# Attention + MoE layer on one core: attention's sums turned by VectorE in 32 by 32 blocks instead of by TensorE

## What is computed

```
xn = layernorm(x)
q, k = rope(xn Wq^T), rope(xn Wk^T);  v = xn Wv^T        # 16 heads of width 8
attn = softmax(q k^T / sqrt(8)) v                          # over the 512 keys of a batch
h    = relu(xn up^T)^2 * combine                           # 32 experts of width 64; combine: top 6 of 32
moe  = h down^T;   shared = relu(xn sup^T)^2 sdown^T       # width 256
out  = x + attn + moe + shared
```

## Time and profile before

| | |
|---|---|
| median of 3 runs | 612.33 us (611.86 to 616.31) |
| the profiled execution, its own time | 611.43 us |
| its span in the trace | 609.6 us |
| TensorE busy | 603.1 us (99%) |
| VectorE, ScalarE, GpSimd busy | 425.5, 407.9, 428.4 us |

### The profile page before, as it was taken

The page is one execution under the profiler, slowest core; times in us unless marked ns, Lnnn a source line. Parts: engine busy times, 40 slices in busy tenths (PEclk is TensorE's granted clock), DMA queues, the critical chain, the costliest instruction groups (busy, mean ns, idle before and its releaser), DMA issues.

```text
span 609.6 us, 20168 instructions
## 1 busy us (share of the span) xinstructions
PE 603.1 (99%) x8269; PEld 269.1 (44%) x8269; DVE 425.5 (70%) x1058; ACT 407.9 (67%) x803; POOL 428.4 (70%) x512
## 2 busy tenths in 40 slices
PE   9999999999999999999999999999999999999997
PEld 7432544444444444434444434454443444444343
DVE  7898965777767776677867778586766877666402
ACT  3578667766776666766667676676667666666664
POOL 5850478677896778867788678876776767667653
PEclk9999999999999999999999999999999999999999
DMA  5176743646446254652437454263544634343430
GB/s 149 32 218 200 165 115 88 216 105 158 111 94 206 59 151 111 205 145 70 122 80 243 106 154 104 68 209 85 140 112 145 191 80 113 75 106 71 106 72 18
DMA packets 52029, 76.19 MB, mean 125 GB/s; under 512 B 5985, under 2 KB 19169, under 8 KB 51937
## 3 DMA queue, kind: packets, MB, share of 16 engines
q1 hardware_dynamic: 51916, 74.90, 45.6%
q10 hardware_dynamic: 20, 0.00, 0.0%
HBM read 56.14 MB, written 18.35 MB: 122 GB/s over the span
## 4 chain that ended last, share of the span: by engine, by line
PE 95%; DVE 2%; DMA 1%; SPq 1%; ACT 0%; issue 0%; DVEq 0%
PE acc L1060 21%; PE pv L1227 20%; PE st L1060 15%; PE upb L1060 10%; PE st L1197 9%; PE sc L1186 6%; PE upb L1197 4%; PE st L1202 3%; PE upb L1202 2%; PE sc L1119 1%; PE st L1169 1%; DVE nmax L930 1%; SPq L361 1%; DMA stacks<-k_stack 1%; DMA k_stack<-qk_parts 1%; PE upb L1169 1%
## 5 line engine op out<-in xcount | busy, mean ns | idle before, releaser
L930 DVE TENSOR_REDUCE nmax<-sc 128x1 f32<-128x512 f32 x512 | 328.5, 686 | 142.7 <-PE sc L1186 131.7
L700 ACT ACTIVATE probs<-st 128x512 f32<-128x512 f32 x359 | 202.8, 595 | 29.1 <-PE st L1202 19.3
L558 POOL TENSOR_TENSOR gated<-gate_at,relu 128x512 f32<-128x512 f32 x111 | 142.0, 1280 | 98.3 <-ACT relu L705 92.0
L562 POOL TENSOR_TENSOR g<-gated,relu 128x512 f32<-128x512 f32 x111 | 142.2, 1281 | 16.2 <-POOL gated L558 0.4
L1202 PE MATMUL st<-stacks 32*128 32x512 f32 x359 | 148.6, 577 | 0.0
L1227 PE MATMUL pv<-probs,v_aug 128*32 128x512 f32 x1024 | 136.4, 605 | 0.1
L1060 PE MATMUL acc<-dn,g 128*32 128x128 f32 x3512 | 134.8, 274 | 0.0
L1186 PE MATMUL sc<-stacks 32*128 32x512 f32 x512 | 132.6, 493 | 0.9 <-DMA stacks<-k_stack 0.4
L1060 PEld LDWEIGHTS acc<-dn,g 128*32 128x32 f32 x3512 | 112.2, 114 | 22.3 <-issue 22.1
L700 ACT ACTIVATE probs<-upb 128x512 f32<-128x512 f32 x153 | 91.0, 595 | 21.0 <-PE st L1202 14.2
L1197 PE MATMUL st<-m_rows,ones 3*128 3x512 bf16 x359 | 99.6, 384 | 0.3 <-ACT sh L682 0.3
(11 more groups left out here) (186 smaller groups left out, 565.4 us busy)
## 6 DMA issues: line engine op xcount, KB each, us to landing
gate_at<-gate_rows SPq DMA_DIRECT2D x62, 512.0 KB, 6.6
stacks<-q_stack SPq DMA_DIRECT2D x30, 256.0 KB, 6.7
stacks<-k_stack SPq DMA_DIRECT2D x30, 256.0 KB, 6.8
q_stack<-qk_parts SPq DMA_DIRECT2D x28, 256.0 KB, 6.6
k_stack<-qk_parts SPq DMA_DIRECT2D x28, 256.0 KB, 5.7
x_res<-in_x SPq DMA_DIRECT2D x8, 256.0 KB, 7.8
out<-y SPq DMA_DIRECT2D x8, 256.0 KB, 7.3
m_rows<-m_parts SPq DMA_DIRECT2D x95, 4.0 KB
```

Source lines behind the costliest of these rows:

```text
L558: nc.gpsimd.tensor_tensor(gated[:, u % 2, :], gate_at[:, group % RING, u % GATES, :], relu[:, u % RELUS, :], ALU.mult).then_inc(gated_read ...
L562: nc.gpsimd.tensor_tensor(g[:, u % 2, :], gated[:, u % 2, :], relu[:, u % RELUS, :], ALU.mult).then_inc(g_ready, 1)
L700: nc.scalar.activation(probs[:, u % 2, h, :], ring_b("st", u * QUAD + h)[:], ACT.Exp).then_inc(probs_ready, 1)
L930: nc.vector.tensor_reduce(out=nmax[:, s % 2, at:at + 1], in_=sc_b[tile % SC_BANKS][:], op=ALU.max, axis=AXX, negate=True).then_inc(s_read, 1)
```

## The change

For the first 15 of the 16 pairs of quads the path over ScalarE, TensorE and the ring is left. VectorE turns the bank `pv` itself, in one `transpose` of 128 by 512 that turns each block of 32 by 32 in place (`turn_att`, in the units n = 0 and 8), and takes the reciprocals of the divisors from the result. A block's turning leaves a head's rows in the partitions of that head's group of 32, and the 128 tokens of a tile in four blocks beside each other. So the division, which must put the tokens on 128 partitions, goes in small products of 32 partitions by 64 elements (4 tiles, 2 quads, 8 columns): four heads by four blocks are sixteen, eight in n = 1 and 9 (heads 0 and 1) and eight in n = 2 and 10 (heads 2 and 3). Each reads a group `h` of 32 partitions, and writes a group `a`; `a` goes from 0 to 3 within a head, so that each product writes another group than the one ahead of it. TensorE's four transposes, their use of the ring and their wide weights, and ScalarE's copy fall away in these 15 places. The last pair stays as it was.

```
 def att_evac(q):                                   # ScalarE, now for the last pair alone
-    if kt == 0 and q and q % PAIR == 0:
-        att_evac(q // PAIR - 1)

+def turn_att(q):                                   # VectorE
+    dve.wait_ge(pv_done, (q + 1) * TT * PAIR)
+    nc.vector.transpose(att_blk[:].rearrange("p t a k c -> p (t a k c)"), pv_b[:]).then_inc(att_ready, 1)
+    dve.wait_ge(att_ready, q + 1)
+    nc.vector.reciprocal(rec_blk[:].rearrange("p t a k -> p (t a) k").unsqueeze(3),
+                         att_blk[:, :, :, :, HD:HD + 1].rearrange("p t a k c -> p (t a) k c")).then_inc(rec_ready, 1)
+
+def att_heads(q, heads):
+    dve.wait_ge(rec_ready, q + 1)
+    j = q * PAIR % NQ
+    if heads[0] == 0 and j == 0:
+        wait(dve, y_ready, q // (NQ // PAIR))
+    for h in heads:
+        src = slice(h * COL, (h + 1) * COL)
+        for a in range(P // COL):
+            last = nc.vector.tensor_tensor(
+                att_y[a * COL:(a + 1) * COL, :, j:j + PAIR, h * HD:(h + 1) * HD],
+                att_blk[src, :, a, :, 0:HD],
+                rec_blk[src, :, a, :].unsqueeze(3).to_broadcast([COL, TT, PAIR, HD]), ALU.mult)
+    last.then_inc(atty_ready, 1)

-                if kt == ATT_KT and q and q % PAIR == 0:
-                    att_out(q // PAIR - 1)
+                if kt < ATT_KT + PAIR and q and q % PAIR == 0:
+                    if kt == 0:
+                        turn_att(q // PAIR - 1)
+                    else:
+                        att_heads(q // PAIR - 1, ((0, 1), (2, 3))[kt - 1])

 def whole(u):                                      # TensorE
-    att = kt == ATT_KT and q and q % PAIR == 0
-    return att or (b + 2 < B and n == (X_UNIT if b else X2_UNIT)) or u == UNITS - 1
+    return (b + 2 < B and n == (X_UNIT if b else X2_UNIT)) or u == UNITS - 1

 def side_work(u):
-    if kt == ATT_KT and q and q % PAIR == 0:
-        att_transpose(q // PAIR - 1)

 def ring_order():
-    if kt == ATT_KT and q and q % PAIR == 0:
-        order += [("att", q // PAIR - 1)]
```

More of the change, by code:

```diff
@@ L149, in build @@
         gT = sb("gT", [NE, T])
-        att_sb = sb("att_sb", [P, T])
-        rec = sb("rec", [P, TT * QUAD, PAIR])
+        att_sb = sb("att_sb", [P, T]); att_blk = sb("att_blk", [P, TT, P // COL, PAIR, PV_STEP])
+        rec = sb("rec", [P, TT * QUAD, PAIR]); rec_blk = sb("rec_blk", [P, TT, P // COL, PAIR])
         att_y = sb("att_y", [P, TT, NQ, QUAD * HD])
@@ L202, in build @@
         pv_done = sem("pv_done"); att_ready = sem("att_ready"); att_turned = sem("att_turned")
-        rec_ready = sem("rec_ready"); atty_ready = sem("atty_ready")
+        rec_ready = sem("rec_ready"); att_last = sem("att_last"); atty_ready = sem("atty_ready")
         v_done = sem("v_done"); v_ready = sem("v_ready")
@@ L714, in att_evac @@
                 act.wait_ge(pv_done, (q + 1) * TT * PAIR)
-                wait(act, att_turned, q)
-                nc.scalar.activation(att_sb[:], pv_b[:], ACT.Copy).then_inc(att_ready, 1)
+                nc.scalar.activation(att_sb[:], pv_b[:], ACT.Copy).then_inc(att_last, 1)
             def side_out(u):
@@ L931, in row_max @@
                                         op=ALU.max, axis=AXX, negate=True).then_inc(s_read, 1)
+            def turn_att(q):
[17 more added lines that the diff above has]
+                last.then_inc(atty_ready, 1)
             def att_out(q):
-                dve.wait_ge(att_turned, q + 1)
-                if q % (NQ // PAIR) == 0:
-                    wait(dve, y_ready, q // (NQ // PAIR))
+                dve.wait_ge(att_turned, 1)
                 a5 = ring_b("att", q)[:].rearrange("p (n k c) -> p n k c", k=PAIR, c=PV_STEP)
@@ L1165, in att_transpose @@
             def att_transpose(q):
-                pe.wait_ge(att_ready, q + 1)
+                pe.wait_ge(att_last, 1)
                 bank_free("att", q)
```

## The result

The changed kernel takes **677.32 us** (median of 4 runs, 674.78 to 681.81) against 612.55 in the runs beside it: ratio 1.105, interval 1.099 to 1.110. The profiled execution took 678.32 us, its span is 676.5. Ratios leave out executions over 1.5% longer than the kernel's fastest, so in two of the experiments the ratio does not match the median beside it.

The account below looks back on a forecast made before the run. TensorE, busy 99%, was taken to bound the kernel, with VectorE's room per unit deciding. Losses of 65.1 us less 6.75 gained gave +58.4 on 611.43: 670 us, range 625 to 702.

Parts of the forecast that it names:

- losses add up: All units: TensorE works in order without another wait to hide late maxima in, so unit losses sum to 65.1 us.
- The gain: TensorE's transposes fall away in 15 places at 0.45 us each, 6.75 us in all.
- The rule (offset - 0.93): A unit whose first maximum starts over 0.93 us after the unit's start loses that offset less 0.93 us.
- The turning: VectorE in n = 0 and 8: one pass, 0.68 us; n = 0 loses 0.16, in batch 6 0.61; its n = 8 0.82.
- The products one after the other, 0.23: VectorE in n = 1, 2, 9, 10: products don't overlap, 0.23 us each, eight last 1.84; held at 0.75.
- GpSimd stops them, and one or two get in between: Products reading two SBUF operands wait for GpSimd's, one or two slipping between its two; meeting held at 0.85, main case 0.60.
- Price of n = 1: Eight products, then the residual: first maximum of the next unit at offset 2.98, a loss of 2.05 us.
- Of n = 2: Eight products, then routing that meets GpSimd's second product: offset 4.35 in the next unit, a loss of 3.42 us.
- Of n = 10: Eight products, then the statistics: offset 3.27, a loss of 2.34 us; without statistics (batches 5 to 7) 1.48.
- n = 9: Eight products with no residual behind them: offset 2.37 in the next unit, a loss of 1.44 us.
- six run ahead of the first product: Products one to six run from -0.51 to 0.87 us around the next unit's start; the seventh waits for GpSimd.
- Batch 7: The sum counted losses there too: 1.44 us for its n = 9 and 1.48 for its n = 10.

Follow-up runs that it names:

- second experiment: The changed kernel with each of the sixteen products writing the group of 32 partitions that it reads: 655.3 us, ratio 1.061 to the kernel before.
- first experiment: The changed kernel with the sixteen products replaced by one-operand reductions of the same size and places, division left out: 653.11 us, ratio 1.065 to the kernel before.

## Why the prediction came out as it did

The time was right: 677.32 against 670, inside 625 to 702, and slower as forecast. The way to it was right in most of its mechanism. One size was too small and one step, that losses add up, did not hold; what the clock cost in its place came out about as large, and that is luck. The [rows] that are put down to batch 3 are of batch 4 when counted from 0, as everywhere else; batches 1 to 5 take the same 71.87 us each, and no price changes by it.

- **The gain**, 15 x 0.45 = 6.75: right. The run without products shows 0.42 to 0.46 each.
- **The rule (offset - 0.93)**: right. Where the clock stays up, offset 3.03 in n = 2 of batch 3 cost 2.09, offset 4.19 in n = 3 a wait of 3.22.
- **The turning**, taken at 0.68 and one pass: 0.70. The first maximum of n = 1 came 0.96 us into the unit, not 1.09, so that the loss of 0.16 was at most 0.02: the routing started 0.27 us after the reciprocals had, with no wait between. In batch 6 the losses were 0.49 (0.61 forecast) and 1.34 (0.82 forecast).
- **The products one after the other, 0.23**: right, 0.22 to 0.24 start to start where GpSimd does nothing beside them. The second experiment shows that the overlap exists, but only inside a group.
- **GpSimd stops them, and one or two get in between**: right; the first experiment shows that two operands are needed for it. Price of n = 1: 2.05, measured waits of 2.05 to 2.12 in batches 2 to 5, but 3.05 and 3.26 in batches 1 and 7, where two products of the eight are stopped. Of n = 2: 3.42, measured 3.22 in batch 3 and 3.0 to 3.2 with the clock kept up ahead of it. Of n = 10: 2.34, measured 2.23 to 2.25 there.
- **n = 9: mis-sized.** 1.44 was the price; the wait is 2.66. VectorE and GpSimd in batch 5:

```profile
488.95 4.10 DVE L945 TENSOR_TENSOR att_y<-att_blk,rec_blk 32x64 f32<-32x64 f32 x8
493.08 2.48 DVE L925 TENSOR_REDUCE nmax<-sc 128x1 f32<-128x512 f32 x4
```

```profile
488.94 0.19 POOL L335 CAST n_parts<-nmax 128x16 bf16<-128x16 f32 x1
...
490.26 1.28 POOL L556 TENSOR_TENSOR gated<-gate_at,relu 128x512 f32<-128x512 f32 x1 [0.28 <-ACT relu L703]
491.69 1.29 POOL L560 TENSOR_TENSOR g<-gated,relu 128x512 f32<-128x512 f32 x1
```

  GpSimd's cut of the maxima, four small pieces from 488.94 on, runs beside the first four products, and these take 0.25 to 0.28 instead of 0.21. So the sixth starts at 490.30, 0.03 behind `gated` instead of ahead of it, and two products wait, the sixth and the eighth. The step "six run ahead of the first product" failed by that much, some 6 us in all. In n = 1 of the same batch the sixth got ahead by 0.01. I had named the cut of the maxima among GpSimd's small pieces and put no price on it.
- **Batch 7: counted where nothing can be lost.** The sum prices n = 9 and 10 of batch 7 as well, at 1.44 and 1.48. TensorE makes no more scores from n = 9 of that batch on, and both units behind, n = 10 and 11, took 4.00 and 3.98 us. So 2.9 us of the 63.1 were forecast for nothing.
- **"Losses add up": failed, through the clock.** I named its fall as the thing that I couldn't price, and expected the loss to grow by it. Its cost is the rest, 25.9 us. But a unit at the lower level is longer, VectorE catches up in it, and the waits of n = 3 and 11 shrink from 37.2 forecast to 6.8 (32.2 when the clock was kept up ahead of them). Wait and rest together are 66.5 against 63.1. That this came out near the forecast is chance: with the clock kept up in n = 2 and 10 the same two are 91.0.

## What to carry to other kernels

Work that moves to an engine with idle time is to be priced unit by unit against the time at which another engine needs it next, not by the busy share: here 8 us more of VectorE's work per batch cost nothing when dealt out by room, and about as much as the forecast said when put in two places. Before small two-operand products go to VectorE, look at where GpSimd's stand, and count what is pushed into them behind your own. When a TensorE that was never idle starts to wait for microseconds, its clock belongs in the sum, and the delays behind it do not simply add.

## What the runs showed of the hardware

- **The clock falls behind single waits in an otherwise full stream.** In the changed kernel it fell to the lower level (1.2 GHz) at waits of 1.89 to 3.26 us, but not at one of 2.06 (batch 3) and not at those from 1.23 to 1.49 (batches 0 and 6). With one operand, waits of 0.9 and 1.2 were never followed by it, one of 1.55 was (batch 0), and those of 3.03 in five of six cases; with products that stay in their group, one of 2.01 was, one of three of 2.26, and those of 2.77 in three of six. Work in the wait that nobody read kept it up in all 14 places. The length of the wait alone thus doesn't decide, and what else does stays open.
- **GpSimd stops VectorE's operations with two operands from SBUF, and not those with one**: 1.2 to 1.3 us instead of 0.21 against at most 0.22, in the same places of the program; the residual, one of whose two operands is in a bank, keeps its 0.69. A small GpSimd piece of 128 by 16 costs such a product some 0.05.
- **A change of the 32 partitions costs about 0.08 us per VectorE instruction** of this size: 0.22 to 0.24 from start to start instead of 0.13 to 0.17.
